# Transformer block on one core: the last batch's output projection in two sums, and the softmax's factor 2^14 on ScalarE

## Reference

```python
qkv = xn @ w_qkv.T + b_qkv                    # 16 heads of 32
scores = q @ k.T / sqrt(32), causal mask
out = softmax(scores) @ v
attention = out @ w_out.T + b_out
ffn = ((silu(xn @ gate_w.T * gate_s) * (xn @ up_w.T * up_s)) @ down_w.T) * down_s   # inner width 1408
```

## Time and profile before

| | |
|---|---|
| median of 3 runs | 1930.7 us (1929.14 to 1932.67) |
| the profiled execution | 1932.21 us |
| its span, first to last instruction | 1930.4 us |
| mean granted clock of TensorE | 0.995 |
| busy: TensorE, VectorE, ScalarE, GpSimd | 97%, 88%, 72%, 34% |

### The profile page before, as it was taken

One profiled execution on the slowest core, in us unless ns is written; L12 is line 12 of the kernel. 1 busy time (PEld: TensorE's weight loads), 2 busy tenths in 40 slices (PEclk: granted clock), 3 DMA queues, 4 the chain that ended last, 5 costly groups with the idle time before them and its releaser, 6 DMA issues.

```text
span 1930.4 us, 35063 instructions
## 1 busy us (share of the span) xinstructions
PE 1872.0 (97%) x11560; PEld 876.3 (45%) x11560; DVE 1705.7 (88%) x5337; ACT 1397.9 (72%) x3801; POOL 647.4 (34%) x593
## 2 busy tenths in 40 slices
PE   7789999999999999999999999999999999999997
PEld 3444444444444444444444444444444444444443
DVE  7999998989898898989989898898989989898893
ACT  5568887777777777777767777777777777777772
POOL 1863342432423424234232423424234242212112
PEclk9999999999999999999999999999999999999999
DMA  8398999997988989888997988989888997977883
GB/s 262 86 177 152 180 180 162 185 160 132 177 130 156 171 149 164 151 153 139 184 158 133 176 134 156 165 156 158 151 138 149 183 154 139 166 121 144 138 159 88
DMA packets 805113, 299.90 MB, mean 155 GB/s; under 512 B 734144, under 2 KB 766912, under 8 KB 804928
## 3 DMA queue, kind: packets, MB, share of 16 engines
q1 hardware_dynamic: 804928, 297.62, 86.5%
HBM read 46.94 MB, written 16.78 MB: 33 GB/s over the span
## 4 chain that ended last, share of the span: by engine, by line
PE 63%; DVE 17%; DMA 8%; SPq 4%; ACT 3%; issue 3%; POOL 2%; ACTq 0%; POOLq 0%; DVEq 0%
PE psW L830 21%; PE psW L805 13%; PE psW L812 8%; PE psW L821 7%; PE psW L838 6%; PE psS L892 5%; DVE PL L1167 4%; PE psW L906 4%; DVE psS L1151 4%; DMA PT<-PL 4%; DMA xin<-in_x 3%; SPq L754 2%; ACT PL L1307 1%; DVE act_t L1145 1%; DVE PL3b L1167 1%
## 5 line engine op out<-in xcount | busy, mean ns | idle before, releaser
L830 PE MATMUL psW<-xT,Wgu 128*128 128x512 f16 x2816 | 670.4, 379 | 6.3 <-DVE PT L1115 4.9
L1293 ACT ACTIVATE psS<-psS,small 128x512 f32<-128x512 f32 (+3 forms) x1024 | 518.9, 511 | 205.4 <-DVE small L1151 203.8
L1151 DVE CUSTOM_DVE_ANT_0 psS<-psS,mask,small 128x512 f32<-128x512 f32 (+3 forms) x1024 | 537.5, 548 | 13.5 <-PE psS L892 12.9
L1383 POOL TENSOR_TENSOR hdn<-act_t,hdn 128x512 f16<-128x512 f32 x176 | 204.4, 1162 | 789.0 <-ACT hdn L1288 789.0
L1167 DVE SCALAR_TENSOR_TENSOR PL<-psS,small,PL 128x256 f16<-128x256 f32 (+3 forms) x896 | 418.7, 513 | 55.2 <-ACT PL L1307 54.4
L1307 ACT ACTIVATE PL<-psS,small 128x256 f16<-128x256 f32 (+3 forms) x896 | 394.8, 512 | 74.5 <-DVE small L1162 45.1
L830 PEld LDWEIGHTS psW<-xT,Wgu 128*128 128x128 f16 x2816 | 270.4, 97 | 302.1 <-DVE PT L1115 5.3
L805 PE MATMUL psW<-xT,Wqkv 128*128 128x512 f16 x1536 | 365.1, 381 | 4.1 <-DVE oT L1171 2.3
L838 PE MATMUL psW<-Wdn,hdn 128*128 128x512 f16 x1408 | 316.5, 379 | 0.3 <-DVE act_t L1138 0.3
L892 PE MATMUL psS<-QK 96*128 96x512 f16 (+3 forms) x1024 | 253.3, 301 | 18.8 <-DVE PL L1167 15.9
L805 PEld LDWEIGHTS psW<-xT,Wqkv 128*128 128x128 f16 x1536 | 146.5, 98 | 168.3 <-issue 4.0
(11 more groups left out here) (151 smaller groups left out, 1716.1 us busy)
## 6 DMA issues: line engine op xcount, KB each, us to landing
QK<-PT SPq DMA_DIRECT2D x192, 256.0 KB, 5.8
y<-in_x SPq DMA_DIRECT2D x68, 256.0 KB, 3.2
out<-y SPq DMA_DIRECT2D x64, 256.0 KB, 3.5
xin<-in_x SPq DMA_DIRECT2D x60, 256.0 KB, 3.7
PT<-PL SPq DMA_TRANSPOSE x224, 5.1
PT<-in_w_qkvT SPq DMA_DIRECT2D x4, 512.0 KB, 6.8
y<-in_downT SPq DMA_DIRECT2D x4, 256.0 KB, 11.3
xT<-in_w_outT SPq DMA_DIRECT2D x4, 256.0 KB, 3.7
```

The source lines that it names most:

```text
L830: mm = e.matmul(ps[:, :], Wgu[:, up, c, 128 * m:128 * (m + 1)], xT[b % 2][:, 4 * xl + c, :], start=(k == 0), stop=last)
L1151: e.tensor_tensor_reduce(s, s, mask[:, 512 - s.shape[1]:512], scale=negsc, scalar=BIG, op0=ALU.add, op1=ALU.min, accum_out=nmax[:, u % 16: ...
L1293: e.activation(s, s, ACT.Exp, bias=nmax[:, u % 16:u % 16 + 1], scale=-1.0, accum_out=rsum[:, u % 16:u % 16 + 1]).then_inc(sem["act exp"], 1)
L1383: e.tensor_tensor(hdn[:, m, 1, :], act_t[plan.gu_units[tuple(k)] % 3][:, :], hdn[:, m, 0, :], op=ALU.subtract).then_inc(sem["pool hl"], 1)
```

## The change

1. The output projections of the last batch (`last_output`) are each split at matmul 9: matmuls 0 to 8 (groups 0 to 2) wait for three of the four `ol`, matmuls 9 to 11 for the fourth. First parts are due 8, 10, 12 and 14 us after the batch's nominal end, second parts 12 us later each. The second part of sum `t` comes behind that of `t - 1`. The fourth sum gets a score bank, that of the last group's seventh cell (`LAST_CELL`), and waits for that cell's `pl`.
2. `late` lets the due times of the last batch's units fall progressively, by up to 6 us at the last unit (`END_EARLY`); `pv`, `oh` and `ol` go with them.
3. `rc2` is a ScalarE `Copy` with scale 2^14 in place of a VectorE `tensor_scalar`. The planned durations of `rc` and `rc2` change from 85 and 85 ns to 100 and 200.

```diff
--- before.py
+++ after.py
@@ -39,7 +39,7 @@
-    "yt": 605, "up": 650, "gate": 610, "rc": 85, "rc2": 85, "ol": 600, "xh": 520, "wqk_hi": (290, 505), "wv_hi": 610, "wo_hi": 610,
+    "yt": 605, "up": 650, "gate": 610, "rc": 100, "rc2": 200, "ol": 600, "xh": 520, "wqk_hi": (290, 505), "wv_hi": 610, "wo_hi": 610,
@@ -60,6 +60,10 @@
 FFW_DN = 65000
 CHK = 40000
 CHK_STEP = 3000
+O_AT = 8000
+O_REST = 12000
+END_EARLY = 6000
+LAST_CELL = len(CELLS) * 4 * NB - NS
 NEVER = 1e15
 SPARE = 100
 SHARED = {"dve": ("nrm0", "ffw", "wqk_lo", "wv_lo", "wo_lo"), "pool": ("nrm", "xl", "hl", "ya", "yb", "ffd")}
@@ -189,7 +193,7 @@
     def begins(self, key):
 
         if key[1] == "mm":
-            return key[2] if key[3] == 0 else None
+            return key[2] if key[3] == 0 and key[2] not in self.banks else None
         if key[1] == "chk":
             return None if ("chk",) in self.banks else ("chk",)
         return key[1:] if key[1] == "pv" else None
@@ -298,6 +302,24 @@
             self.add(end + 6000, "sp", ("yl", n + 4), ("sp", "ys", n))
             self.add(end + 12000, "pool", ("yb", n + 4), ("sp", "yl", n + 4), ("dve", "bias"))
 
+    def last_output(self, due, t):
+
+        b, n = NB - 1, 4 * (NB - 1) + t
+        item = "o", b, t
+        if t == 3:
+            self.banks[item] = NW + LAST_CELL % NS
+        for m in range(12):
+            late = [("turn", "pe", "mm", item, m - 1)] if m else [("dve", "ol", 4 * b + 2), ("dve", "wo_lo", 3), ("pool", "ya", n)]
+            if m in (0, 9) and t:
+                late.append(("turn", "pe", "mm", ("o", b, t - 1), m + 2 if m else 8))
+            if m == 0 and t == 3:
+                late.append(("dve", "pl", cell_units(LAST_CELL)[-1]))
+            if m == 9:
+                late.append(("dve", "ol", 4 * b + 3))
+            self.add(due + 2000 * t + (0.01 * m if m < 9 else O_REST), "pe", ("mm", item, m), *late)
+        self.add(due + O_REST, "dve", ("yf", b, t), ("pe", "mm", item, 11), ("pool", "ya", n))
+        self.add(due + O_REST, "sp", ("ys", n), ("dve", "yf", b, t))
+
     def gate_up(self, due, b, m):
         k = b, m
         x_there = [self.transposed(4 * b + t) for t in range(4)]
@@ -343,7 +365,8 @@
 
     def late(self, u):
 
-        return max(0, LATE * (1 - u / LATE_UNITS))
+        last = 64 * (NB - 1)
+        return max(0, LATE * (1 - u / LATE_UNITS)) - max(0, END_EARLY * (u - last) / 64)
 
     def scores(self, u):
         G = u // 16
@@ -357,12 +380,12 @@
         if u != units[-1]:
             return
         self.chain(due + 1500, "dve", ("rc", u), ("act", "exp", u))
-        self.chain(due + 1500, "dve", ("rc2", u), ("dve", "rc", u))
+        self.chain(due + 1500, "act", ("rc2", u), ("dve", "rc", u))
         for v in units:
             i, h = ORDER[v % 16]
             before = G - 2 if i == 3 else G - 1
             free = [("sp", "pt", before, i)] if before >= 0 else [("pe", "chk", i ^ 1)] * (i >= 2) if G == 0 else [PE_BIAS, ("pe", "chk", 4)]
-            self.chain(due + 2000, "act", ("ph", v), ("dve", "rc2", u), *free)
+            self.chain(due + 2000, "act", ("ph", v), ("act", "rc2", u), *free)
         for v in units:
             i, h = ORDER[v % 16]
             self.chain(due + 2600, "dve", ("pl", v), ("act", "ph", u))
@@ -477,7 +500,7 @@
                 self.normal(begin + (8 + 15 * t) * 1000, 4 * (b + 1) + t)
         else:
             for t in range(4):
-                self.output(begin + 64 * UNIT + 20000 + 2600 * t, b, t)
+                self.last_output(begin + 64 * UNIT + O_AT, t)
 
 
 def sp_buffer(step, n=0, *k):
@@ -652,7 +675,7 @@
         return at[engine, *step]
 
     def tile(item):
-        return psW[plan.banks[item]]
+        return (psW + psS)[plan.banks[item]]
 
     def bank_emptied(item):
 
@@ -816,8 +839,12 @@
                     if k == 0:
                         for n in range(4):
                             pe.wait_ge(*done("dve", "wo_lo", n))
-                        for n in range(4):
+                        for n in range(3 if b == NB - 1 else 4):
                             pe.wait_ge(*done("dve", "ol", 4 * b + n))
+                        if b == NB - 1 and t == 3:
+                            pe.wait_ge(*done("dve", "pl", cell_units(LAST_CELL)[-1]))
+                    elif k == 9 and b == NB - 1:
+                        pe.wait_ge(*done("dve", "ol", 4 * b + 3))
                     mm = e.matmul(ps[:, :], oT[:, (4 * b + g) % 5, xl, 128 * t:128 * (t + 1)], Wout[wl][:, g, :], start=(k == 0), stop=last)
                 elif kind in ("ga", "up"):
                     b, m = key
@@ -1155,11 +1182,6 @@
                     part = slice(units[0] % 16, n % 16 + 1)
                     dve.wait_ge(*done("act", "exp", n))
                     e.reciprocal(rinv[:, part], rsum[:, part]).then_inc(sem["dve rc"], 1)
-                elif step == "rc2":
-                    units = cell_units(cell(n))
-                    part = slice(units[0] % 16, n % 16 + 1)
-                    dve.wait_ge(*done("dve", "rc", n))
-                    e.tensor_scalar(rinv[:, part], rinv[:, part], 2.0 ** 14, None, op0=ALU.mult).then_inc(sem["dve rc2"], 1)
                 elif step == "pl":
                     i, h = ORDER[n % 16]
                     out = PLv[pl_tile(n // 16, i)]
@@ -1292,10 +1314,15 @@
                     act.wait_ge(*done("dve", "max", cell_units(cell(u))[-1]))
                     e.activation(s, s, ACT.Exp, bias=nmax[:, u % 16:u % 16 + 1], scale=-1.0,
                                  accum_out=rsum[:, u % 16:u % 16 + 1]).then_inc(sem["act exp"], 1)
+                elif step == "rc2":
+                    units = cell_units(cell(n))
+                    part = slice(units[0] % 16, n % 16 + 1)
+                    act.wait_ge(*done("dve", "rc", n))
+                    e.activation(rinv[:, part], rinv[:, part], ACT.Copy, scale=2.0 ** 14).then_inc(sem["act rc2"], 1)
                 elif step == "ph":
                     i, h = ORDER[n % 16]
                     before = n // 16 - (2 if i == 3 else 1)
-                    act.wait_ge(*done("dve", "rc2", cell_units(cell(n))[-1]))
+                    act.wait_ge(*done("act", "rc2", cell_units(cell(n))[-1]))
                     if before >= 0:
                         act.wait_ge(*done("sp", "pt", before, i))
                     elif n // 16 == 1:
```

## The result

The kernel after takes 1902.25 us (median of 4, 1900.19 to 1904.4) against 1930.9; the ratio is 0.9854 (0.9839 to 0.9869). The predicted direction was right, and so was the size of the gain at the end of the kernel; the gain before the end was about 20 us where the prediction took 4.

A forecast was written before the change was run, and what follows sets the result against it. VectorE was taken to bound 50 to 235 us, TensorE the batches after, and TensorE's waits the end. From 1932.2 us, less 6.8 (end), 4 (body) and 1.5 (profiled run to median), it forecast 1920, range 1912 to 1928.

The forecast's parts named there:

- the density of the stores: After the last matmul: four stores issued within 2.4 us end 0 to 2 us later than a lone one; 0.8 taken.
- the 4.78 us: TensorE's idle time after the last down projection, until the last group's fourth transpose lands; early output-projection matmuls were to fill it.
- a reserve: Last batch: due times up to 6 us earlier may start the last transposes 4.9 us earlier, but change nothing more.
- rival three: Whole body: ScalarE's chain becomes the late one, delaying `ph`, `pl` and score matmuls; slower, above 1934.6 us; chance 0.09.
- 11.3 us are at stake: From 235 to 1890 us: TensorE's 18 waits, all score matmuls waiting for a `pl`; 1 us of gain taken.
- the 4.7 us of `pl` waits: Before 235 us: small-half score matmuls waiting for `pl`, the largest waits the change can touch; 3 us of gain taken.
- 18 + 11 gained: Upper bound on the body's gain: 18 us in the first stage plus 11 after it; 4 us taken.
- the forecast's own range: Whole kernel: 1915 to 1924 us, from a tail gain of 4.1 to 7.6 and a body gain of 1 to 8.
- relief of busy time: VectorE throughout: moving the 640 `rc2` away frees 99.1 + 36.6 us of its busy time.
- Rival one: Body: VectorE's relief stays hidden, gain 0, leaving only the end's 6.8 us, so 1923.9 us; chance 0.23.
- rival two: First stage, 50 to 235 us: follows VectorE, 14 us or more of 23 come back, 1910 or below; chance 0.09.
- Rival four: End: early sums do little because planned times place them badly, and a longer body cancels it; 1927 to 1931; chance 0.12.

The follow-up runs named there:

- durations_only: Kernel before with only the planned durations of `rc` and `rc2` changed from 85 and 85 to 100 and 200, `rc2` still on VectorE: 1937.56 us.
- factor_left_out_same_order: Kernel after with every list in its order, but the 640 ScalarE multiplications by 2^14 not issued: 1901.93 us.
- five pairs: `rc2` on VectorE against on ScalarE under five settings of planned durations, four with the split, one without: ScalarE faster by 6.4 to 26.6 us.
- The spare instructions: Kernel after, same order, plus 640 VectorE instructions nobody waits for, right behind `rc`: reciprocals 1904.48 us, multiplications by 2^14 1922.24 us.
- five orders on ScalarE with the split: Kernel after and the same with planned `rc`, `rc2` of 85/85, 90/90, 100/150, 85/210: 1902.25, 1915.96, 1916.33, 1905.89, 1906.14 us.
- one_column_each: Kernel before, order unchanged, each two-column `rc2` issued as two one-column multiplications on VectorE: 1926.37 us.
- vector_100_150: Split alone, `rc2` on VectorE, with planned durations of `rc` and `rc2` at 100 and 150: 1930.57 us.

## Why the prediction was wrong

**The end: the size right, the way to it in part luck.** Split sums before `pv`, no idle time, `pv` at the higher clock: as said. The net gain from the last down projection on is 6.2 us (6.8 predicted); the density of the stores costs 1.5 us (0.8 taken, bounds 0 to 2). But the prediction let the early sums fill the 4.78 us and called the earlier due times a reserve that changes nothing more. In the kernel after the earlier `pv` of group 62, which it named as possible, had closed that gap already, and an order without the split ends as early (18.5 us in `durations_only` against 18.3): the 1.5 us that the split then fills are about what its denser stores cost. Taking only the due times back cost 1.8 us at the end and 0.9 in the last batch by the traces. Either step fills the same gap, so the sum came out.

**The cost on ScalarE: the right form, a size too high.** 0.26 us was taken; 0.211 on average was measured, just under the lower bound of 0.216, 135 us in all where 166 was taken and 192 named in rival three. It fits in and costs nothing at the end, as `factor_left_out_same_order` shows. Rival three, with the page of the Trainium skill (ScalarE: Activation LUTs, Rules for kernel authors) that puts multiplications on VectorE, is refuted here: ScalarE's busy time rose by 73 us and the kernel got faster in all five pairs.

**The body: the step that failed.** "In the 1655 us after it 11.3 us are at stake; I take 1" and "the 4.7 us of `pl` waits ... I take 3 us". Measured are 20.4 us by the starts of the matmuls, 9.2 before 230 us and 11.2 after. Two things were wrong. Of the stake a small share was taken, by the argument that a new order brings waits of its own: by the idle time that the prediction went by, 15.4 us came back where 4 was taken. And the stake was read from named waits and from windows, which hide gaps under 0.16 us: the excess after 230 us was 25.6 us, not 11.3, and 5.0 us more came back beyond the idle time. The 20 us lie within the bounds that the prediction gave the body (18 + 11 gained), but its range, 1912 to 1928, did not reach that far. (A slip in it: with a tail of 4.1 and a body of 1 the forecast's own range ends at 1925.6, not 1924.) The row on which the other answer hung was there: the 18.21 us that 58 `rc2` held in a stage where VectorE is the bound, and the 36.9 us of waits for GpSimd. The prediction called these relief of busy time, and took it at 136 us; VectorE's busy time fell by 90 (100 or more was its sign), because in the profile these instructions overlap their neighbours on VectorE. The spare instructions show what they were: a wait in the middle of VectorE's list, which makes the next `max` and `pl` late; 640 instructions without the wait cost 2 us, with it 20. That holds in the order of the kernel after; in that of the kernel before, the waits were worth 4 to 5 us. The Trainium skill (SBUF — State Buffer, Terms, "shared port pair") states the lock; the trace agrees for the two-column form (end 0.02 us after GpSimd's), and the one-column form and the reciprocal were long only 3 times in all runs, each time right behind another VectorE instruction that was.

**Rival one**, relief hidden, is refuted; **rival two** was nearest (first stage 8 to 9 us better, not 14), but the 11 us after 230 us were in none of the rivals. **Rival four** did not occur.

**What stays open.** How the 19 us of the move divide. The waits for GpSimd account for 4 to 5 us in one order and 18 in another. The rest in the former would be the place of a step that waits for its neighbour on the same engine, and the order drawn with it; this was not separated: no run has `rc2` itself on VectorE in the order of the kernel after. The kernel after lies 7 us under the mean of the five orders on ScalarE with the split (1909.3), but only 2.5 under the mean of the three planned with 150 ns or more (1904.8); how much of the 7 is a good draw and how much the plan's knowledge of the duration is open.

## What to carry to other kernels

Where VectorE works beside GpSimd, look at the spread of its shortest instructions, not at their sum: a few that end with GpSimd's instruction delay every step behind them. Another engine, or a form that does not wait, can then be worth more than the time saved; how much more depended here on the order (4 to 18 us). Where a planner lays out the order, draw some orders before and after an edit and compare those, since one draw moved this kernel by up to 14 us, and gave the end without a split almost all that the split was made for. Before crediting a step that fills a wait, look whether the wait is still there. To size what a saturated TensorE can still win, sum the distances between matmul starts, not the idle time of a page that shows overlapping matmuls.

## What the runs showed of the hardware

A multiplication of a 128x2 f32 tile on VectorE waited for a running GpSimd instruction (up to 1.6 us, end 0.02 us after it), also when its two columns had a gap between them; a 128x1 one (1 long in 1024, 0.34 us, in `one_column_each`) and a reciprocal of either width (0.19 us at most, but for one of 0.36 us in `vector_100_150`) did not, except right behind a VectorE instruction that was long itself. A ScalarE `Copy` on one or two columns took 0.21 us. Four stores of 256 KB issued within 2.3 us ended 5.2 us after the last `yf`, a lone one 3.7.
